# Cross-attention on one Trainium2 core: the four weighted-sum blocks of a batch moved into one block of the next iteration

## The chip, the cores and the metric

The kernel runs on one core of a Trainium2 chip (trn2). The metric is the device time of one execution in microseconds, as the median of several runs. The profile shows one execution by itself; its own time and its span are given beside the median below.

## The reference, cut to what matters

One pre-norm decoder layer in float32 on x of shape (32, 100, 256): self-attention (16 heads of 64), cross-attention to a context of (32, 361, 256) (16 heads of 16), and a routed feed-forward layer with 8 experts. The change is in cross-attention alone, which computes for each of the 32 batches:

```python
q = split_heads(h @ Wq.T + bq)      # h = layernorm(x): 100 rows, 16 heads of 16
k = split_heads(ctx @ Wk.T + bk)    # 361 rows
v = split_heads(ctx @ Wv.T + bv)
scores = einsum('bhqd,bhkd->bhqk', q, k) / sqrt(16)
attn = softmax(where(mask == 0, -inf, scores))
out = einsum('bhqk,bhkd->bhqd', attn, v)
x = x + out.reshape(B, 100, 256) @ Wo.T + bo
```

## The kernel before

The kernel is one program with stages in a row: self-attention, `cross_attention`, routing, `experts`. Each engine runs its own instruction stream, ordered by hand, and the streams meet through semaphores. In `cross_attention` all five streams loop over the 32 batches with `over_batches` (L1529): batches 0 and 1 and the last four are written out, 2 to 27 run in a loop of two batches a turn.

The loop is a software pipeline. In its step for batch b the TensorE stream (`step`, L1457) makes

- the keys and queries of batch b + 2 (`keys` L1354 in two halves, `queries` L1345) and, at the end, the transposed input of batch b + 3 (`turn_x`);
- the scores of batch b + 1, one head at a time (`scores` L1382, called by `maximum_of`), 100 queries by 362 keys in one matmul, only so that VectorE can take the row maxima. They alternate between two PSUM banks, and head h waits for the maximum of head h - 2 (L1385);
- the shifted and transposed scores of batch b (`shifted` L1390), from which ScalarE makes the probabilities with an exponential (`exps` L1130). There are 12 of these tiles a batch: four quarters of heads (u = 0 to 3) by three blocks of keys (kt = 0 to 2). They alternate between two PSUM banks too. The negated maxima enter as a row of the queries by a DMA that ScalarE issues (`maxima` L1119); the shifted scores of quarters 0 and 2 wait for it (L1393);
- the values of batch b + 1 in three blocks (`values` L1364);
- the weighted sums (`weighted` L1401): for a quarter of heads, three key blocks by four heads, each a small matmul with 32 columns of weights that writes one of four groups of 32 PSUM partitions. The profile shows a quarter's 12 calls as 24 matmuls;
- the output of batch b - 1 (`turn_raw`, `turn_out`, `project`).

The weighted sums of quarter 0, 1 and 2 of batch b stand in its own step, behind heads 6, 10 and 14 of the next batch's scores; quarter 3 of batch b - 1 stands in step b behind the transposed maxima. The probabilities lie in two buffers, quarter u in buffer u % 2, so the exponentials of a quarter wait for the weighted sums of two quarters before (L1132).

VectorE (`step`, L1286) takes the 16 row maxima (L1244), and between them the low bits of keys (L1227) and queries (L1234), layer-norm statistics (L1214, L1217), the quotients (L1253, L1255), the normalised input (L1222), the routing statistics (L1268) and the residual (L1262), in a fixed order. ScalarE makes high bits of keys (L1107) and queries, exponentials and copies. GpSimd splits the context of batch b + 3 into high and low bits (`split_context`, L1036 and L1038) once the values of batch b + 1 are done; the keys need it (L1357). SP stores the packed keys and queries of batch b + 2 to DRAM and loads them back in two halves (`place`, L1007); heads 0 and 8 wait for a half each (L1384).

Of the kernel before, what the change touches and what calls it, by code (L numbers as in the profile page):

```python
# [11 lines left out]
ACT = mybir.ActivationFunctionType  # L12
AX_X = mybir.AxisListType.X

B, S, D = 32, 100, 256
# [19 lines left out]
KT = [121, 121, 119]  # L35
# [62 lines left out]
def reach(eng, semaphore, value):  # L98

    if isinstance(value, int) and value <= 0:  # L100
        return
    eng.wait_ge(semaphore, value)
# [691 lines left out]
def cross_attention(nc, c, ctxT, wo, bo, kb_dram, kd, qd, ones_dram):  # L794
# [12 lines left out]
    with ExitStack() as ctx:  # L807
        def sb(name, shape, dt=F32):
            return ctx.enter_context(nc.sbuf_tensor(name, shape, dt))

        def psum(name, shape, dt=F32):
            return ctx.enter_context(nc.psum_tensor(name, shape, dt))

        def sem(name):
            return ctx.enter_context(nc.semaphore(name))

        KP = KT[0]
# [19 lines left out]
        v_ext = sb("v_ext2", [KP, 2, 3, H2, 32])  # L837
        row_max = sb("row_max2", [S, 2, H2])
        neg_max = sb("neg_max", [HG, 2, S], F32R)
        probs = sb("probs2", [KP, 2, 3, 4 * S])  # L840
        recip = sb("recip2", [S, H2])
        o_raw = sb("o_raw", [128, 4 * S])
        o_norm = sb("o_norm2", [S, D])
# [4 lines left out]
        ps_t = [psum(f"psb_t{i}", [128, 512]) for i in range(2)]  # L848
# [42 lines left out]
        pv_ready = sem("pv2_ready")  # L891
# [51 lines left out]
        def more(b, ahead):  # L943
            return not isinstance(b, int) or b + ahead < B
# [141 lines left out]
        def _(act):  # L1086
# [42 lines left out]

            def exps(b, u, kt):  # L1130
                if kt == 0:
                    reach(act, pv_ready, b * 4 + (u - 1))  # L1132
                i = 3 * u + kt
                act.wait_ge(shifted_ready, b * 12 + (i + 1))
                act.sem_inc(act_passed, 1)
                act.activation(probs[0:KT[kt], u % 2, kt], ps_t[i % 2][0:KT[kt], 0:4 * S], ACT.Exp,  # L1136
                               scale=HD2 ** -0.5).then_inc(probs_ready, 1)

            def raw_out(b):
# [191 lines left out]
        def _(pe):  # L1331
# [13 lines left out]
            def queries(b, p):  # L1345
                bank_free(pe, b, Q0)
                pe.wait_ge(xt_copied, fill_of(b, Q0) + 1)
                for g in range(KD):
                    for k in range(KD):
                        ins = pe.matmul(bank(p, Q0)[:, S * g:S * (g + 1)], wq_sb[:, k, 128 * g:128 * (g + 1)],  # L1350
                                        x_t[:, S * k:S * (k + 1)], start=(k == 0), stop=(k == KD - 1))
                ins.then_inc(q_filled, 1)

            def keys(b, p, g):  # L1354
                bank_free(pe, b, KEYS[g])
                if g == 0:
                    pe.wait_ge(c_lo_ready, fill_of(b, K0) + 1)  # L1357
                for k in range(KD):
                    cols = slice(128 * g, 128 * (g + 1))
                    ins = split3(pe, bank(p, KEYS[g])[:, 0:S2E], wk_hi[:, k, cols], wk_lo[:, k, cols],  # L1360
                                 c_hi[:, p, k], c_lo[:, p, k], k == 0, k == KD - 1)
                ins.then_inc(k_filled, 1)
# [10 lines left out]
            def turn_maxima(b, p, half):  # L1373

                f = MT1 if half else MT0
                n, par = fill_of(b, f), p if half else 1 - p
                bank_free(pe, b, f)
                pe.wait_ge(max_ready, n * H2 + (HG * half + HG))
                pe.transpose(bank(p, f)[0:HG, 0:S], row_max[:, par, HG * half:HG * (half + 1)],
                             c.ident[0:S, 0:S]).then_inc(mt_filled, 1)  # L1380

            def scores(b, p, h):  # L1382
                if h % HG == 0:
                    pe.wait_ge(packed[p][h // HG], (b - p) * (PACKS * 8) + PACKS * 16)  # L1384
                reach(pe, max_ready, b * H2 + (h - 1))  # L1385
                u, g, a = h // 4, h // 2 % 2, h % 2
                pe.matmul(ps_s[h % 2][0:S, 0:S2E], q2[0:97, p, u, g, S * a:S * (a + 1)], k2[0:97, p, u, g],  # L1387
                          start=True, stop=True).then_inc(scores_ready, 1)

            def shifted(b, p, u, kt):  # L1390
                i, n = 3 * u + kt, KT[kt]
                reach(pe, probs_ready, b * 12 + (i - 1))
                if i % 6 == 0:  # L1393
                    pe.wait_ge(max_placed[i // 6], b * 16 + 16)
                rows = slice(KT0[kt], KT0[kt] + n)
                for g in range(2):
                    ins = pe.matmul(ps_t[i % 2][0:n, 2 * S * g:2 * S * (g + 1)], k2[:, p, u, g, rows], q2[:, p, u, g],  # L1397
                                    start=True, stop=True)
                ins.then_inc(shifted_ready, 1)

            def weighted(b, p, u):  # L1401
                if u == 0:
                    reach(pe, raw_copied, b)
                    pe.wait_ge(v_copied, b * 3 + 3)
                    pe.wait_ge(live_ready, b + 1)
                for kt in range(3):
                    pe.wait_ge(probs_ready, b * 12 + (3 * u + kt + 1))
                    n = KT[kt]
                    for h in range(4):
                        ins = pe.matmul(ps_o[32 * h:32 * (h + 1), S * u:S * (u + 1)], v_ext[0:n, p, kt, 4 * u + h, :],  # L1410
                                        probs[0:n, u % 2, kt, S * h:S * (h + 1)], start=(kt == 0), stop=(kt == 2))
                ins.then_inc(pv_ready, 1)

            def turn_raw(b):
                pe.wait_ge(raw_copied, b + 1)
                reach(pe, x2_ready, b)
                for u in range(4):
                    ins = pe.transpose(ps_f[0:S, 128 * u:128 * (u + 1)], o_raw[:, S * u:S * (u + 1)], c.ident[:])
                ins.then_inc(raw_turned, 1)
# [37 lines left out]
            def step(b, p):  # L1457
                first = isinstance(b, int) and b == 0
                nxt, next2 = more(b, 1), more(b, 2)

                def maximum_of(*heads):
                    for h in heads:
                        if nxt:
                            scores(b + 1, 1 - p, h)

                shifted(b, p, 0, 0)
                if next2:
                    keys(b, p, 0)
                maximum_of(0)
                shifted(b, p, 0, 1)  # L1470
                if next2:
                    queries(b, p)
                maximum_of(1)
                shifted(b, p, 0, 2)
                if next2:
                    keys(b, p, 1)
                maximum_of(2)
                turn_maxima(b, p, 1)
                if not first:
                    weighted(b - 1, 1 - p, 3)  # L1480
                maximum_of(3)
                shifted(b, p, 1, 0)
                maximum_of(4)
                shifted(b, p, 1, 1)
                maximum_of(5)
                shifted(b, p, 1, 2)
                maximum_of(6)
                weighted(b, p, 0)
                maximum_of(7)
                if not first:  # L1490
                    turn_raw(b - 1)
                shifted(b, p, 2, 0)
                maximum_of(8)
                if nxt:
                    values(b, p, 0)
                shifted(b, p, 2, 1)
                maximum_of(9)
                if nxt:
                    turn_maxima(b, p, 0)
                    values(b, p, 1)  # L1500
                shifted(b, p, 2, 2)
                maximum_of(10)
                weighted(b, p, 1)
                if not first:
                    turn_out(b - 1)
                maximum_of(11)
                shifted(b, p, 3, 0)
                if nxt:
                    values(b, p, 2)
                maximum_of(12)  # L1510
                shifted(b, p, 3, 1)
                maximum_of(13)
                if not first:
                    project(b - 1)
                if more(b, 3):
                    turn_x(b, p)
                shifted(b, p, 3, 2)
                maximum_of(14)
                weighted(b, p, 2)
                maximum_of(15)  # L1520

            over_batches(pe, step)
            weighted(B - 1, 1, 3)
            turn_raw(B - 1)
            turn_out(B - 1)
            project(B - 1)
# [2 lines left out]
def over_batches(eng, emit):  # L1529

    emit(0, 0)
    emit(1, 1)
    with eng.Fori(1, B // 2 - 2) as i:
        emit(i * 2, 0)
        emit(i * 2 + 1, 1)
    for b in range(B - 4, B):
        emit(b, b % 2)
# [635 lines left out]
```

## Time and profile before

| | |
|---|---|
| median of 3 runs | 1639.34 us (1637.56 to 1639.75) |
| the profiled execution | 1636.23 us |
| its span, first to last instruction | 1634.5 us |
| mean granted TensorE clock | 0.947 of full speed |
| TensorE matmuls busy | 1444.6 us (88%) |
| VectorE busy | 963.9 us (59%) |
| ScalarE busy | 758.2 us (46%) |
| GpSimd busy | 557.3 us (34%) |
| cross-attention in the span | about 690 to 1218 us |

PE is TensorE's matmuls, PEld its weight loads, DVE VectorE, ACT ScalarE, POOL GpSimd, SP the queue that issues most DMAs. Tiles go by the program's names with the buffer numbers left out: `psb_s` are the scores' banks, `psb_t` those of the shifted scores, `psb_o` the weighted sums, `psb_p` the projections. Lines L52 to L54 are the three matmuls of a split-precision product: with `wk` among the operands they are keys, with `wv` values. In a timeline a row starts with the time from the span's start and the duration, both in us; "x24" means 24 instructions merged, and the bracket gives the idle time of the engine before it and what ended it.

### The profile page before, as it was taken

The page shows a single profiled execution, that of the slowest core. Times are in us where ns is not written, and L with a number is a line of the kernel's source. Part 1 is how long each engine was busy: PE and PEld are TensorE (multiplying, and loading weights), DVE is VectorE, ACT ScalarE, POOL GpSimd, SP SyncE. Part 2 cuts the span into 40 slices and gives each one's busy share as a digit, 9 for nine tenths or more (in the row PEclk, how much of TensorE's full clock was granted, in tenths as well). Part 3 has the DMA queues.
Part 4 walks back from the last instruction along what each step waited for, and adds up shares of the span by engine and source line. Part 5 has one row for each costly group of instructions (what it writes and reads, how often), then busy time and mean ns, then how long its engine had stood idle before and what let it go on. Part 6 is the DMA issues. An engine that isn't in the chain of part 4 may idle for free. (4 is left out here: it accounts for less than half of the span.)

```text
span 1634.5 us, 39265 instructions
## 1 busy us (share of the span) xinstructions
PE 1444.6 (88%) x12244; PEld 1249.5 (76%) x12244; DVE 963.9 (59%) x2371; ACT 758.2 (46%) x1830; POOL 557.3 (34%) x690
## 2 busy tenths in 40 slices
PE   4899899999999999599999999999977029999997
PEld 3688878888787878578888888888867028888886
DVE  5647474756666655367777777777752225555553
ACT  4547474646555565146555555555541002222221
POOL 5244343525252616322222222222201443333332
PEclk9999999999999999689999999999995559999999
DMA  5813030303021211377676667676621514555551
GB/s 183 238 25 82 1 80 0 80 10 70 22 59 30 50 41 43 98 200 187 190 185 189 186 189 188 186 191 184 177 58 49 151 53 157 178 173 189 183 184 52
DMA packets 160098, 195.82 MB, mean 120 GB/s; under 512 B 83742, under 2 KB 128453, under 8 KB 159782
## 3 DMA queue, kind: packets, MB, share of 16 engines
q1 hardware_dynamic: 154504, 186.19, 41.5%
q0 software_dynamic: 3968, 6.59, 1.3%
q10 hardware_dynamic: 1568, 2.30, 0.5%
q8 instruction: 32, 0.52, 0.1%
q14 instruction: 26, 0.21, 0.0%
HBM read 138.67 MB, written 58.11 MB: 120 GB/s over the span
## 5 line engine op out<-in xcount | busy, mean ns | idle before, releaser
L1244 DVE TENSOR_REDUCE row_max<-psb_s 100x1 f32<-100x361 f32 x512 | 263.4, 531 | 140.3 <-PE psb_s L1387 134.4
L1136 ACT ACTIVATE probs<-psb_t 121x400 f32<-121x400 f32 (+1 forms) x384 | 190.3, 507 | 114.7 <-PE psb_t L1397 112.0
L1387 PE MATMUL psb_s<-k,q 97*100 97x362 f32 x512 | 185.4, 364 | 15.4 <-DVE row_max L1244 9.5
L510 POOL TENSOR_TENSOR diag<-neg_ident,row_max 100x400 fp32r<-100x400 f32 x128 | 112.0, 896 | 184.3 <-DVE row_max L603 153.9
L1397 PE MATMUL psb_t<-q,k 98*121 98x200 f32 (+1 forms) x768 | 147.1, 274 | 2.1 <-ACT probs L1136 1.7
L2079 PE MATMUL psd_y<-w_sb,hid 128*128 128x256 f32 x640 | 144.5, 379 | 0.0
L2071 PE MATMUL psd_h<-h_in,w_sb 128*128 128x256 f32 x640 | 143.0, 382 | 1.4 <-ACT h_in L1937 1.4
L2071 PEld LDWEIGHTS psd_h<-h_in,w_sb 128*128 128x128 f32 x640 | 122.6, 192 | 18.6 <-issue 1.8
L2079 PEld LDWEIGHTS psd_y<-w_sb,hid 128*128 128x128 f32 x640 | 120.1, 190 | 15.5
L1397 PEld LDWEIGHTS psb_t<-q,k 98*121 98x121 f32 (+1 forms) x768 | 125.4, 184 | 6.2 <-ACT probs L1136 2.7
L1387 PEld LDWEIGHTS psb_s<-k,q 97*100 97x100 f32 x512 | 86.0, 168 | 41.4 <-DVE row_max L1244 27.4
L1952 ACT ACTIVATE hid<-psd_h,b_sb 128x256 f32<-128x256 f32 x100 | 47.3, 473 | 146.0 <-PE psd_h L2071 146.0
L426 ACT ACTIVATE probs<-ps_t 100x400 f32<-100x400 f32 x128 | 57.5, 501 | 111.7 <-PE ps_t L751 111.7
L1410 PE MATMUL psb_o<-probs,v_ext 121*32 121x100 f32 (+1 forms) x3072 | 92.5, 253 | 0.0
L1912 POOL DMA_INDIRECT out<-res,token x40 | 40.9, 1023 | 151.3 <-DVE res L2039 145.2
L292 ACT COPY q_t<-ps_p 64x200 f32<-64x200 f32 x112 | 57.0, 509 | 73.4 <-PE ps_p L54 72.6
L52 PE MATMUL ps_p<-x_lo,w_hi 128*128 128x400 f32 x224 | 82.6, 369 | 4.7 <-DVE q_t L292 0.6
L496 POOL CAST o_hi<-stage 128x400 fp32r<-128x400 f32 x64 | 59.1, 924 | 76.9 <-ACT stage L436 40.8
L1937 ACT ACTIVATE h_in<-psd_x,bet,gam 128x256 f32<-128x256 f32 x40 | 20.4, 560 | 139.6 <-PE psd_x L2051 139.6
L436 ACT COPY stage<-ps_ot 64x200 f32<-64x200 f32 x256 | 81.8, 320 | 6.0 <-PE ps_ot L761 1.2
L603 DVE TENSOR_REDUCE row_max<-ps_s 100x4 f32<-100x400 f32 x128 | 67.6, 571 | 28.4 <-PE ps_s L707 27.9
L498 POOL TENSOR_TENSOR o_lo<-stage,o_hi 128x400 fp32r<-128x400 f32 x64 | 81.9, 1280 | 5.1
(226 smaller groups left out, 3596.1 us busy)
## 6 DMA issues: line engine op xcount, KB each, us to landing
w_sb<-in_w SPq DMA_DIRECT2D x40, 1024.0 KB, 7.7
packed_keys<-k_st SPq DMA_DIRECT2D x32, 724.0 KB, 3.6
k<-packed_keys SPq DMA_DIRECT2D x64, 362.0 KB
v_rows<-v_tok SPq DMA_DIRECT2D x32, 400.0 KB
v_ext<-v_rows SPq DMA_DIRECT2D x32, 400.0 KB
q<-packed_queries SPq DMA_DIRECT2D x64, 200.0 KB
k<-packed_keys SPq DMA_DIRECT2D x64, 181.0 KB
packed_queries<-q_st SPq DMA_DIRECT2D x128, 50.0 KB, 2.6
```

What stands on the lines that cost most here:

```text
L52: pe.matmul(out, hi_l, lo_r, start=first, stop=False)
L436: act.copy(*turned_part(r - 2, a, odd)).then_inc(ot_copied_act, 1)
L498: pool.tensor_tensor(lo, src, hi.bitcast(F32), ALU.subtract).then_inc(o_lo_ready, 1)
L510: pool.tensor_tensor(diag[:, g % 2], c.neg_ident[0:S, 0:S].unsqueeze(1).to_broadcast([S, GH, S]), row_max[:, g // 2 % 2, g % 2].unsqueeze( ...
L603: dve.reduce_max(row_max[:, r % 2, :, 2 * n:2 * n + 2].rearrange("p g h -> p h g"), ps_s[n][0:S, :].rearrange("p (h j) -> p h j", h=2)[:, ...
L1136: act.activation(probs[0:KT[kt], u % 2, kt], ps_t[i % 2][0:KT[kt], 0:4 * S], ACT.Exp, scale=HD2 ** -0.5).then_inc(probs_ready, 1)
L1244: dve.reduce_max(row_max[:, p, h:h + 1], ps_s[h % 2][0:S, 0:S2], AX_X).then_inc(max_ready, 1)
L1387: pe.matmul(ps_s[h % 2][0:S, 0:S2E], q2[0:97, p, u, g, S * a:S * (a + 1)], k2[0:97, p, u, g], start=True, stop=True).then_inc(scores_ready, 1)
L1397: ins = pe.matmul(ps_t[i % 2][0:n, 2 * S * g:2 * S * (g + 1)], k2[:, p, u, g, rows], q2[:, p, u, g], start=True, stop=True)
L1410: ins = pe.matmul(ps_o[32 * h:32 * (h + 1), S * u:S * (u + 1)], v_ext[0:n, p, kt, 4 * u + h, :], probs[0:n, u % 2, kt, S * h:S * (h + 1)], ...
L2071: ins = pe.matmul(ps_h[f % 4][:, 0:T], c.w1_sb[:, p, k, 128 * f:128 * (f + 1)], h_in[:, p, k], start=(k == 0), stop=(k == KD - 1))
L2079: ins = pe.matmul(ps_y[t][:, 0:D], hid[:, f, 128 * t:128 * (t + 1)], c.w2_sb[:, p, f, :], start=(f == 0), stop=(f == NF - 1))
```

## The change

The four quarters' weighted sums of batch b - 1 now stand together in step b, right behind head 0's scores; after the last batch its four quarters follow together. Each quarter has a probabilities buffer of its own, so the exponentials of quarter u wait for the weighted sums of the same quarter of the batch before.

```diff
-        probs = sb("probs2", [KP, 2, 3, 4 * S])
+        probs = sb("probs2", [KP, 4, 3, 4 * S])
...
             def exps(b, u, kt):
                 if kt == 0:
-                    reach(act, pv_ready, b * 4 + (u - 1))
+                    reach(act, pv_ready, b * 4 + (u - 3))
...
-                act.activation(probs[0:KT[kt], u % 2, kt], ps_t[i % 2][0:KT[kt], 0:4 * S], ACT.Exp,
+                act.activation(probs[0:KT[kt], u, kt], ps_t[i % 2][0:KT[kt], 0:4 * S], ACT.Exp,
...
-                                        probs[0:n, u % 2, kt, S * h:S * (h + 1)], start=(kt == 0), stop=(kt == 2))
+                                        probs[0:n, u, kt, S * h:S * (h + 1)], start=(kt == 0), stop=(kt == 2))
...
                 maximum_of(0)
+                if not first:
+                    for u in range(4):
+                        weighted(b - 1, 1 - p, u)
                 shifted(b, p, 0, 1)
...
                 turn_maxima(b, p, 1)
-                if not first:
-                    weighted(b - 1, 1 - p, 3)
                 maximum_of(3)
...
                 maximum_of(6)
-                weighted(b, p, 0)
                 maximum_of(7)
...
                 maximum_of(10)
-                weighted(b, p, 1)
                 if not first:
                     turn_out(b - 1)
...
                 maximum_of(14)
-                weighted(b, p, 2)
                 maximum_of(15)

             over_batches(pe, step)
-            weighted(B - 1, 1, 3)
+            for u in range(4):
+                weighted(B - 1, 1, u)
             turn_raw(B - 1)
```

## Rows read from the trace of the kernel before

**Rows 1.** The page's first part: busy us, share of the span, instructions.

```profile
PE 1444.6 (88%) x12244; PEld 1249.5 (76%) x12244; DVE 963.9 (59%) x2371; ACT 758.2 (46%) x1830; POOL 557.3 (34%) x690
```

**Rows 2.** Windows, all of cross-attention: stretch, busy by engine (PE, PEld, DVE, ACT, POOL), clock, DMA.

```profile
690.00:1218.00 528.00, 512.10 (x5958) 434.54 (x5959) 370.21 (x843) 305.36 (x787) 119.71 (x180) 0.99 0.67 181
```

**Rows 3.** List of waits, 720 to 1200 us: total us, times, longest.

```profile
PEld psb_s L1387 <- DVE row_max L1244: 20.6, 60, 0.4
```

**Rows 4.** PE's timeline: one steady batch, and one row of batch 30.

```profile
900.58 0.33 PE L1387 MATMUL psb_s<-k,q 97*100 97x362 f32 x1
900.75 0.36 PE L1397 MATMUL psb_t<-q,k 98*121 98x200 f32 x2
...
903.59 0.72 PE L1410 MATMUL psb_o<-probs,v_ext 121*32 121x100 f32 x24
...
906.22 0.72 PE L1410 MATMUL psb_o<-probs,v_ext 121*32 121x100 f32 x24
...
910.75 0.72 PE L1410 MATMUL psb_o<-probs,v_ext 121*32 121x100 f32 x24
...
912.00 0.29 PE L52 MATMUL psb_p<-wv_lo,c_hi 128*119 128x256 f32 x1
...
914.53 0.33 PE L1387 MATMUL psb_s<-k,q 97*100 97x362 f32 x1
914.79 0.72 PE L1410 MATMUL psb_o<-probs,v_ext 121*32 121x100 f32 x24
...
915.69 0.36 PE L1397 MATMUL psb_t<-q,k 98*121 98x200 f32 x2
915.89 0.34 PE L52 MATMUL psb_p<-c_lo,wk_hi 128*128 128x362 f32 x1
...
916.92 0.33 PE L1387 MATMUL psb_s<-k,q 97*100 97x362 f32 x1
...
1198.57 0.43 PE L1397 MATMUL psb_t<-q,k 98*121 98x200 f32 x2 [0.34 <-DMA q<-neg_max]
```

**Rows 5.** Windows, second keys to head 7's scores: batch 0, then a steady batch.

```profile
707.60:712.22 4.62, 3.92 (x44) 2.97 (x42) 3.97 (x11) 2.88 (x8) 0.27 (x2) 1.00 0.20 44
902.20:907.07 4.87, 4.57 (x69) 3.48 (x67) 4.11 (x11) 3.27 (x9) 0.34 (x2) 1.00 0.84 211
```

**Rows 6.** DVE's timeline: batch 0 (709 to 710), then a steady batch.

```profile
709.55 0.58 DVE L1227 SCALAR_TENSOR_TENSOR k_st<-psb_p,stage,k_st 128x362 fp32r<-128x362 f32 x1
710.05 0.96 DVE L1244 TENSOR_REDUCE row_max<-psb_s 100x1 f32<-100x361 f32 x2
...
904.17 0.58 DVE L1227 SCALAR_TENSOR_TENSOR k_st<-psb_p,stage,k_st 128x362 fp32r<-128x362 f32 x1
904.81 0.97 DVE L1244 TENSOR_REDUCE row_max<-psb_s 100x1 f32<-100x361 f32 x2
905.70 0.42 DVE L1214 BATCH_NORM_STATS2 stats<-x_all 100x6 f32 x1
...
906.48 0.97 DVE L1244 TENSOR_REDUCE row_max<-psb_s 100x1 f32<-100x361 f32 x2
```

**Rows 7.** PEld's timeline (weight loads), the same steady batch.

```profile
907.07 0.16 PEld L1387 LDWEIGHTS psb_s<-k,q 97*100 97x100 f32 x1 [0.35 <-DVE row_max L1244]
...
914.79 0.50 PEld L1410 LDWEIGHTS psb_o<-probs,v_ext 121*32 121x32 f32 x24 [0.18 <-issue]
```

**Rows 8.** PE's timeline at the end of cross-attention: quarters 2 and 3 together.

```profile
1215.93 1.24 PE L1410 MATMUL psb_o<-probs,v_ext 121*32 121x100 f32 x48
```

**Rows 9.** POOL's timeline, the same steady batch: the split of the context.

```profile
914.01 1.59 POOL L1038 TENSOR_TENSOR c_lo<-c_t,c_hi 128x722 fp32r<-128x722 f32 x1
```

**Rows 10.** PE's timeline, batch 0: third value block, then the next keys.

```profile
716.68 0.29 PE L52 MATMUL psb_p<-wv_lo,c_hi 128*119 128x256 f32 x1
...
720.35 0.41 PE L52 MATMUL psb_p<-c_lo,wk_hi 128*128 128x362 f32 x1 [0.27 <-POOL c_lo L1038]
```

**Rows 11.** Windows, the same columns as rows 2: the DMA queues when a steady batch ends.

```profile
914.00:914.60 0.60, 0.60 (x7) 0.53 (x5) 0.34 (x2) 0.09 (x1) 0.59 (x1) 1.00 0.00 0
```

## The prediction

> **What bounds the kernel now.** I read the page first, then the windows of the cross-attention stage, the list of waits, and last the timelines of one batch. The page's engine line [rows 1] gives TensorE 88% of the span. Inside cross-attention it is busier still: 512 of 528 us, at a clock share of 0.99 [rows 2]. The Trainium skill ("Trainium Kernel Development and Optimization", Performance Expectations) calls matmul busy time a bad measure, because matmuls are pipelined; the trace agrees, since 4.57 us of a 4.87 us stretch count as busy [rows 5] although weight loads stand idle in it. So a busy TensorE may still be waiting, and I went on to the waits. TensorE's weight loads wait 20.6 us in all for VectorE's row maxima [rows 3], always in the same part of a batch. From one batch to the next, head 0's score matmul goes from 900.58 to 916.92 [rows 4]: 16.34 us a batch, 32 batches.
>
> A batch has two kinds of stretch. From the second key matmuls (902.20) to head 7's scores (907.07), 4.87 us [rows 5], VectorE sets the pace: its low bits of the keys start at 904.17, two maxima follow at 904.81, the batch-norm statistics at 905.70, two maxima at 906.48 [rows 6], and head 7's scores start at 907.07, after 0.35 us of idleness that ended with a maximum [rows 7]. The scores have two banks, so head 7 must wait for head 5's maximum (L1385). Everywhere else TensorE works nearly without a pause and sets the time.
>
> The four weighted blocks stand at 903.59 (quarter 3 of the batch before), 906.22 (quarter 0), 910.75 and 914.79 (quarters 1 and 2) [rows 4]. **The first two lie in VectorE's stretch, the last two in TensorE's.**
>
> **What a block costs.** Alone: from head 14's scores (914.53) to the shifted scores (915.69) is 1.16 us [rows 4]; it holds two score matmuls at 0.17 each (900.58 to 900.75), so the block takes 0.83 on TensorE with both its transitions. I use the same for quarter 1. A second block behind another: the kernel's end has the only pair, 48 matmuls in 1.24 us [rows 8] where 24 take 0.72 [rows 4], so 0.52 us. Four in one block: 0.83 + 3 x 0.52 = 2.39 us. Its 192 instructions in a row are not seen before; the pair is the nearest row, and I take its rate. The bounds are 0.52 and 0.83 for each further one.
>
> Why a lone block is dearer: its weight load starts with its first matmul at 914.79, after 0.18 us idle [rows 7], where other loads run ahead. The Trainium skill ("TensorEngine Tiling (Array Packing)", Tiling Modes, Key Properties) has the rule: changing the tiling mode drains the array. The trace agrees with it: 0.83 against 0.52 is 0.31 a switch. By that rule alone three switches a batch would go and the change would win; the rows below speak against it.
>
> **The change, part by part, for batches 1 to 29:**
>
> 1. The block of four goes in behind head 0's scores, before the second shifted scores. That is TensorE's own stretch (900.58 to 902.20 holds no wait): **+2.39 us**. Its operands are long ready, the last probabilities being from the batch before.
>
> 2. Quarters 3 and 0 leave VectorE's stretch. TensorE has 1.66 us less to do there, but the chain of VectorE starts with the second keys and stays: keys (TensorE), high bits (ScalarE), low bits, two maxima, statistics, maximum, head 7's scores. The first batch is the test that the old kernel contains: it has no quarter 3 in that stretch, and its stretch still takes 4.62 us against 4.87 [rows 5]. The 0.25 comes from head 3's maximum, which there starts 0.50 us behind the low bits (709.55, 710.05) and 0.64 in the steady batch (904.17, 904.81) [rows 6], and from small pauses. So **-0.25**, not -1.66. Quarter 0 in that first stretch is then cover that TensorE waits behind anyway; bounds: 0 and -1.66. What is late next is nothing new: the same VectorE chain, with TensorE idle some 1.9 us in it instead of 0.5.
>
> 3. Quarter 1 leaves TensorE's stretch: **-0.83**. VectorE idles behind it, and its consumers (raw copy, quotients) now belong to the batch before and are early.
>
> 4. Quarter 2 leaves the stretch from the third value block (912.00) to the first keys of the next batch (915.89), 3.89 us [rows 4]. Without it TensorE would need 3.06. But GpSimd splits the next context there, only after that value block: its subtraction starts at 914.01 and takes 1.59, to 915.60 [rows 9]. In the first batch that chain did decide: value block at 716.68, keys at 720.35 after a wait of 0.27 for it [rows 10], 3.67 us. So the stretch can shrink to 3.67 only: **-0.22**, not -0.83. The wait of 0.61 is new, with the keys and all scores behind it. Bounds: -0.83 and 0.
>
> 5. ScalarE's first exponential now waits for the block's first quarter (the four buffers make it wait for quarter 0 of the batch before, which is read some 1 us after it would start). Behind it on ScalarE stands the copy of the keys' high bits, and behind that VectorE's low bits; TensorE needs them only for the second keys (their bank), which come behind the block's 2.39 us. That covers it: 0. Uncovered it would cost about that 1 us a batch.
>
> 6. DMA: no transfer is added. But stores of queries and keys, and so the load of the first half of the packed keys, start 2.39 us later in the batch, on SP's queue too, where the loads of the second half are behind them. In the old kernel the DMA queues are empty from 914.00 [rows 11] and head 0 of the next batch starts at 916.92, 2.9 us on. The batch grows by 1.1, so the spare falls to about 1.6: 0. The negated maxima of the first half come for the next shifted scores; a late one costs at most what step 4 does not hide. In the last batch but one such a wait shows already, 0.34 [rows 4]. Probability buffers take more space and no time.
>
> Sum for a batch: 2.39 - 0.25 - 0.83 - 0.22 = **+1.09 us; x 29 = +31.6**. Batch 0 has no block and already waits for the split: -0.83. Batch 30 has no keys or statistics; its quarters 3 and 0 lie before the wait for the maxima's DMA (the 0.34): 2.39 - 2 x 0.83 = +0.73. Behind batch 31 the end becomes four blocks instead of two (+1.04), in front of it stand 2.39, and one of its own blocks was in the way: together +2.6. **Total +34.1 us.** The profiled execution took 1636.2 (span 1634.5 and 1.7 around it), so 1670.3 for it; it lies 3.1 below the median of the runs, 1639.34. On the median: **1673.4**.
>
> **Rivals.** *The switches decide (faster).* If heads 3 to 7 are not held by VectorE once the blocks are out, all four lone blocks (3.32) turn into 2.39: -0.93 a batch; with the split's wait +0.61 that is -0.32, in all 1630 us; without it 1611. For it: TensorE counts as busy through the stretch. Against: the first batch's 4.62 and the 0.35 us idles. It decides if more than 1.34 of the 1.66 us come back from that stretch. 6%. *No measurable change:* VectorE's chain gives back about 1.1 us more than I take, in 29 batches, about 1640; the first batch shows nothing like it. 4%.
> *The split is hidden:* quarter 2 gives its whole 0.83, so +0.48 a batch: 1656. Against: 3.67 was measured. 8%.
> *The packed keys come late:* the load now meets the second half's traffic; 2 us later than I say costs 0.4 us a batch, 1685. For it: a DMA share of 0.84 in the stretch at 902 [rows 5]. 10%.
> *The long block is not fed:* each further quarter costs between 0.52 and 0.83, at the middle +0.46 a batch, 1687, at the end 1702. Against: the pair ran at the full rate. 6%.
> *The change does not do what it says* has no room here: the blocks move, visibly.
>
> **The numbers.** The forecast, with 66%, has a range of its own of 1662 to 1683 (errors of 0.35 us a batch in steps 2 and 4). With the hidden split below and the late keys above, 1655 to 1690 holds a little over 8 in 10. About 0.2% (3 us) is what a measurement of this kernel can tell from no change. Slower by more than that: 66 + 8 + 10 + 6 = 90%; within it 4%; faster 6%.
>
> **What would show it.** One group of 96 matmuls of the weighted sums a batch, about 2.3 us long (step 1). From the second keys to head 7's scores 4.6 to 4.9 us, with the waits of TensorE's weight loads for the row maxima up from 0.7 to about 2 us a batch (step 2). From the third value block to the first keys 3.7 us, and a new wait of TensorE for GpSimd's split of some 0.6 us a batch (step 4). A batch of 17.4 us. The forecast is wrong if the stretch to head 7 falls under 4 us, if the block takes 2.7 us or more, or if a wait for the packed keys shows.

## The result and the profile after

The changed kernel takes **1688.46 us** in the median (4 runs, 1686.11 to 1692.84) against 1638.45 for the kernel before in the same comparison: ratio 1.0308, 95% interval 1.0285 to 1.0331, so 50 us slower. The forecast was 1673.4, slower by 34, with a range to 1690: the sign and the mechanism held, the size was a third too small.

For the changed kernel, the page's engine line and the windows of the stretch from the second keys to head 7's scores in two batches in a row (columns: stretch, its length, busy PE, PEld, DVE, ACT, POOL, clock, DMA share, GB/s):

```profile
PE 1463.6 (87%) x12244; PEld 1269.3 (75%) x12244; DVE 958.2 (57%) x2371; ACT 750.5 (44%) x1830; POOL 557.0 (33%) x690
...
906.39:911.08 4.69, 3.49 (x20) 2.50 (x18) 4.01 (x11) 3.26 (x9) 0.34 (x2) 1.00 0.39 97
925.24:929.94 4.70, 3.50 (x21) 2.52 (x19) 4.02 (x11) 3.27 (x9) 0.35 (x2) 1.00 0.47 102
```

These answer to [rows 5]: the stretch still takes 4.70 us, although TensorE is now busy for 3.50 of it instead of 4.57. VectorE is busy for 4.02 us of it, where it was 4.11. TensorE's timeline of two changed batches, with the transposes of maxima (L1379) that mark a batch's length:

```profile
907.57 0.25 PE L1379 MATMUL psb_p<-ident,row_max 100*8 100x100 f32 x1
...
916.47 0.29 PE L52 MATMUL psb_p<-wv_lo,c_hi 128*119 128x256 f32 x1
...
920.12 0.43 PE L52 MATMUL psb_p<-c_lo,wk_hi 128*128 128x362 f32 x1 [0.37 <-POOL c_lo L1038]
...
921.22 0.33 PE L1387 MATMUL psb_s<-k,q 97*100 97x362 f32 x1
921.48 2.28 PE L1410 MATMUL psb_o<-probs,v_ext 121*32 121x100 f32 x96
923.69 0.46 PE L1397 MATMUL psb_t<-q,k 98*121 98x200 f32 x2
...
925.24 0.34 PE L52 MATMUL psb_p<-c_lo,wk_hi 128*128 128x362 f32 x1
926.43 0.25 PE L1379 MATMUL psb_p<-ident,row_max 100*8 100x100 f32 x1
...
929.94 0.42 PE L1387 MATMUL psb_s<-k,q 97*100 97x362 f32 x1 [0.56 <-DVE row_max L1244]
...
934.05 0.29 PE L52 MATMUL psb_p<-wv_lo,c_hi 128*119 128x256 f32 x1
...
944.07 0.25 PE L1379 MATMUL psb_p<-ident,row_max 100*8 100x100 f32 x1
```

Cut at the same instructions as [rows 4], a batch before and a batch after (from the third values at 916.47 to those at 934.05) compare like this (us; the last column is what the prediction's steps made of each part):

| part of a batch | before | after | predicted |
|---|---|---|---|
| head 0's scores and the block of four | 0.17 | 2.47 | 2.56 |
| to the second keys | 1.45 | 1.55 | 1.45 |
| second keys to head 7's scores | 4.87 | 4.70 | 4.62 |
| head 7's scores to the third values | 4.93 | 4.11 | 4.10 |
| third values to the first keys | 3.89 | 3.65 | 3.67 |
| first keys to head 0's scores | 1.03 | 1.10 | 1.03 |
| sum | 16.34 | 17.58 | 17.43 |

So all of the predicted terms are there. What no step had stands in the length of the batches: 926.43 to 944.07 is 17.64, but 907.57 to 926.43 is **18.86**, and so is every fourth batch of this execution. Windows of the same work, from the first to the third shifted scores of quarter 2, in a long and in a short batch:

```profile
911.69:915.56 3.87, 3.87 (x22) 3.72 (x20) 2.71 (x7) 1.50 (x4) 0.70 (x2) 0.56 0.87 243
930.55:933.14 2.59, 2.58 (x23) 2.27 (x20) 2.56 (x7) 1.44 (x4) 0.69 (x2) 1.00 0.91 290
```

The same matmuls take 3.87 us instead of 2.59, and the granted clock is 0.56 instead of 1.00: nearly the whole of this stretch ran at 1.2 GHz instead of 2.4. Seven batches of the steady part have such a fall, always right behind the stretch in which TensorE idles; the kernel before has none there. Together they are 7 x 1.25 = 8.8 us of the profiled execution. That execution is also the slowest of the four runs. Three more falls, and a wait for the packed keys at head 0's scores of batch 31, belong to the stage's end; the wait in TensorE's timeline:

```profile
1242.50 0.41 PE L1387 MATMUL psb_s<-k,q 97*100 97x362 f32 x1 [1.53 <-DMA k<-packed_keys]
```

Last, the list of waits of the changed kernel, 720 to 1200 us:

```profile
PEld psb_s L1387 <- DVE row_max L1244: 47.6, 83, 1.0
DVE k_st L1227 <- ACT k_st L1107: 33.8, 27, 1.5
...
ACT probs L1136 <- PE psb_o L1410: 74.9, 27, 3.4
...
PEld psb_t L1397 <- DMA q<-neg_max: 7.6, 18, 0.7
...
PE psb_p L52 <- POOL c_lo L1038: 6.8, 20, 0.8
```

TensorE's weight loads wait 47.6 us for row maxima where [rows 3] had 20.6, with 83 waits instead of 60. ScalarE's wait for the block (74.9) and VectorE's behind it (33.8) are new and large; whether they cost anything is tried below. The wait for GpSimd's split is the one of step 4. The one for the negated maxima's DMA, 18 times in 27 batches, is new as well: the list of the kernel before has a single one, of 0.3 us.

### The profile page after: what moved, and what is told of

Its sections match the earlier page's. It is cut to its first block and busy times, and to the rows that moved or that the text cites. A ratio compares the mean times of both kernels' runs of the same rounds, so it can differ in the third digit from the quotient of the medians.

```text
span 1691.1 us, 39395 instructions
## 1 busy us (share of the span) xinstructions
PE 1463.6 (87%) x12244; PEld 1269.3 (75%) x12244; DVE 958.2 (57%) x2371; ACT 750.5 (44%) x1830; POOL 557.0 (33%) x690
## 5 line engine op out<-in xcount | busy, mean ns | idle before, releaser
L1244 DVE TENSOR_REDUCE row_max<-psb_s 100x1 f32<-100x361 f32 x512 | 257.3, 529 | 158.7 <-PE psb_s L1387 150.2
L1387 PE MATMUL psb_s<-k,q 97*100 97x362 f32 x512 | 177.8, 369 | 41.3 <-DVE row_max L1244 37.5
L1397 PE MATMUL psb_t<-q,k 98*121 98x200 f32 (+1 forms) x768 | 156.2, 286 | 6.2 <-ACT probs L1136 2.3
L1951 ACT ACTIVATE hid<-psd_h,b_sb 128x256 f32<-128x256 f32 x100 | 47.4, 474 | 147.2 <-PE psd_h L2070 146.0
L1044 POOL TENSOR_SCALAR var_eps<-mv 100x1 f32<-100x1 f32 x32 | 7.5, 236 | 277.8 <-DVE mv L1217 277.8
```

What stands on the lines that cost most here:

```text
L1244: dve.reduce_max(row_max[:, p, h:h + 1], ps_s[h % 2][0:S, 0:S2], AX_X).then_inc(max_ready, 1)
```

## The experiments

Times are medians; "a batch" is read from the transposes of maxima in each trace. The kernel before was timed again with each group of runs (medians 1638.45 to 1640.16), and the ratios compare within a group; a difference between medians of two groups is known to some 2 us only.

### Old places, four buffers

```diff
-        probs = sb("probs2", [KP, 2, 3, 4 * S])
+        probs = sb("probs2", [KP, 4, 3, 4 * S])
...
-                    reach(act, pv_ready, b * 4 + (u - 1))
+                    reach(act, pv_ready, b * 4 + (u - 3))
```

(and `u` for `u % 2` in the two uses; the blocks stay where they were)

> The kernel before with four probabilities buffers and the exponentials' later wait, the blocks left in their old places. My theory (the place of the blocks decides, the buffers do nothing): 1639 us, a batch of 16.3. Rival (the larger buffers or the other wait of ScalarE cost something by themselves): 1645 or more.

Measured 1637.48 us, ratio 0.9998 (0.9983 to 1.0013), a batch of 16.3:

```profile
901.65 0.25 PE L1379 MATMUL psb_p<-ident,row_max 100*8 100x100 f32 x1
...
917.95 0.25 PE L1379 MATMUL psb_p<-ident,row_max 100*8 100x100 f32 x1
```

The buffers do nothing by themselves; the place of the blocks is the whole loss.

### The block in VectorE's stretch

```diff
                 maximum_of(0)
-                if not first:
-                    for u in range(4):
-                        weighted(b - 1, 1 - p, u)
                 shifted(b, p, 0, 1)
...
                 shifted(b, p, 1, 1)
+                if not first:
+                    for u in range(4):
+                        weighted(b - 1, 1 - p, u)
                 maximum_of(5)
```

With four buffers the engines would wait for each other for ever (the third shifted scores need the first exponential, and that needs the block), so there are eight: quarter u of batch b in buffer 4 (b % 2) + u.

> The block of four stands behind the shifted scores of quarter 1's second key block, inside the stretch that VectorE paces, instead of behind head 0's scores; eight probabilities buffers make that order possible. Theory of the stretches: from the second keys to head 7's scores about 5.4 us (VectorE's chain runs beside the block), 5.4 - 4.70 = +0.7 there and -2.3 in TensorE's own stretch, so 17.6 becomes 16.0 a batch, and without the idle time there is no fall of the clock: about 1625 to 1635 us, at or below the kernel before. Rival (a long block costs what it costs wherever it stands, because of its instructions or the clock): it stays near 1688.

Measured 1647.48 us, ratio 1.0048 (1.0025 to 1.0071): 41 us less than the changed kernel, with the same instructions in the same block of four. A batch takes 16.5, and the steady part has no fall of the clock but one, at 753 us. TensorE's timeline of the stretch, and its window:

```profile
880.09 0.38 PE L52 MATMUL psb_p<-c_lo,wk_hi 128*128 128x362 f32 x1
...
882.19 0.41 PE L1390 MATMUL psb_s<-k,q 97*100 97x362 f32 x1 [0.26 <-DVE row_max L1247]
...
882.73 2.28 PE L1413 MATMUL psb_o<-probs,v_ext 121*32 121x100 f32 x96
884.95 0.40 PE L1390 MATMUL psb_s<-k,q 97*100 97x362 f32 x1
...
886.09 0.41 PE L1390 MATMUL psb_s<-k,q 97*100 97x362 f32 x1 [0.37 <-DVE row_max L1247]
```

```profile
880.09:886.09 6.00, 5.36 (x117) 4.58 (x115) 4.02 (x11) 3.08 (x9) 1.53 (x4) 1.00 0.90 246
```

The block adds 6.00 - 4.70 = 1.3 us here and took 2.3 in front. I had expected 0.7: VectorE finishes its queue at 884.2, and head 5's scores (884.95), issued only after the block, restart it only at 885.50, after 1.31 us of idleness; so two waits of TensorE (0.26 before the block, 0.37 after) stay. The rival, that a long block costs the same anywhere, is out. The forecast of 1625 to 1635, at or below the kernel before, was missed for that 0.6 a batch.

### Statistics early

```diff
                 if more(b, 2):
                     keys(b + 2, p, 0)
+                if more(b, 3):
+                    norm_stats(b + 3)
                 if nxt:
                     maxima(b + 1, 1 - p, 1, 2)
...
                     maxima(b + 1, 1 - p, 3, 5)
-                if more(b, 3):
-                    norm_stats(b + 3)
```

(in VectorE's stream, on top of the change)

> The changed kernel with VectorE's batch-norm statistics moved out of its chain, to behind the first keys' low bits, where VectorE idles beside the block. Theory (VectorE's chain sets the stretch from the second keys to head 7): the stretch goes from 4.70 to about 3.9 us, -0.8 a batch, some 25 us, and with less idle time also fewer falls of the clock: 1655 to 1665. Rival (TensorE or ScalarE sets that stretch): no change, 1688.

Measured 1668.02 us, ratio to before 1.0172 (1.0149 to 1.0195), 20 us less than the changed kernel, and no fall of the clock in the steady part:

```profile
900.12 0.25 PE L1379 MATMUL psb_p<-ident,row_max 100*8 100x100 f32 x1
...
917.16 0.25 PE L1379 MATMUL psb_p<-ident,row_max 100*8 100x100 f32 x1
```

This batch took 17.04, the steady ones 17.09 on average. Not one instruction of TensorE was touched: VectorE's chain sets the stretch. It gave 0.53 a batch rather than 0.8, about 15 of the 20 us; the rest goes with the falls of the clock. TensorE's wait of 0.56 in front of head 7 is gone; those in front of heads 4 and 5 (0.23 and 0.33, in the changed kernel 0.22 and 0.33) do not hang on the statistics and stay.

### The idle time filled

```diff
+            def fill(b, n):
+                if isinstance(b, int) and b == 0:
+                    return
+                reach(pe, x2_ready, b - 1)
+                for _ in range(n):
+                    pe.transpose(ps_f[:, 0:S], c.neg_ident[0:S, :], c.ident[0:S, 0:S])
...
                 shifted(b, p, 1, 0)
+                fill(b, 2)
                 maximum_of(4)
                 shifted(b, p, 1, 1)
+                fill(b, 3)
                 maximum_of(5)
+                fill(b, 1)
                 shifted(b, p, 1, 2)
                 maximum_of(6)
+                fill(b, 6)
                 maximum_of(7)
```

> The changed kernel with 12 transposes of a constant (about 0.11 us each, results unused) put where TensorE idles before heads 4, 5 and 7; they add work and take none away. Theory that the idle time brings the clock down (one batch in four has 3.41 us at half clock and takes 18.87 instead of 17.6): the falls inside the steady batches vanish, all take 17.6 to 17.7, and the time falls by 5 to 10 us in spite of the added work. Rival (the falls come from something else, or the added work is paid for): the falls stay and the time rises by up to 1.3 x 30 = 39 us.

Measured 1679.18 us (1677.71 to 1679.83), ratio to before 1.0240 (1.0219 to 1.0261): 9.3 us less than the changed kernel, with 372 useless matmuls more. TensorE's timeline of the stretch:

```profile
901.80 0.34 PE L52 MATMUL psb_p<-c_lo,wk_hi 128*128 128x362 f32 x1
...
903.49 0.34 PE L1419 MATMUL psb_f<-ident,neg_ident 100*128 100x100 f32 x2
903.88 0.41 PE L1387 MATMUL psb_s<-k,q 97*100 97x362 f32 x1
...
904.33 0.42 PE L1419 MATMUL psb_f<-ident,neg_ident 100*128 100x100 f32 x3
...
905.07 0.25 PE L1419 MATMUL psb_f<-ident,neg_ident 100*128 100x100 f32 x1
...
905.74 0.68 PE L1419 MATMUL psb_f<-ident,neg_ident 100*128 100x100 f32 x6
906.50 0.41 PE L1387 MATMUL psb_s<-k,q 97*100 97x362 f32 x1
```

901.80 to 906.50 is 4.70 us, as without the filling: so much of TensorE's time in this stretch is free. That is step 2 of the prediction laid bare. And the falls are gone from the steady part. Windows of 770 to 1220 us in this run, in the changed kernel, and in the run below with a shorter split and no filling:

```profile
770.00:1220.00 450.00, 436.26 (x5143) 377.28 (x5142) 294.70 (x686) 238.72 (x637) 102.82 (x154) 1.00 0.64 172
```

```profile
770.00:1220.00 450.00, 411.63 (x4711) 353.87 (x4711) 290.94 (x678) 236.93 (x628) 99.62 (x150) 0.97 0.63 170
```

```profile
770.00:1220.00 450.00, 417.24 (x4849) 361.78 (x4847) 297.08 (x690) 241.20 (x640) 77.93 (x153) 0.97 0.65 173
```

### Eight buffers

The changed kernel with the eight buffers of the second experiment; `reach(act, pv_ready, b * 4 + (u - 7))`.

> The changed kernel with eight probabilities buffers, so that ScalarE's first exponential of a batch no longer waits for the block (it stands idle 2.7 us there, and the high bits of the first keys behind it). My step 5 says that the block covers this wait: no change, 1688, a batch of 17.6. Rival (the wait delays keys and maxima and is part of the loss): 0.2 us a batch or more come back, 1680 or less.

Measured 1688.45 us, ratio 1.0310 (1.0284 to 1.0336): the changed kernel's time. (The four runs of each spread over 7 to 8 us, so that the medians agree to 0.01 us is luck.) The 75 us of ScalarE's waits for the block are gone from the list, and nothing comes back. The largest new wait of the profile costs nothing, as step 5 had it.

### The split cut short

```diff
-            pool.memset(c_lo[:, :, :, S2:S2E].bitcast(F32), 0.0).then_inc(pad_ready, 1)
+            pool.memset(c_lo[:, :, :, 120:S2E].bitcast(F32), 0.0).then_inc(pad_ready, 1)
...
-                pool.tensor_tensor(c_lo[:, p, :, 0:S2], c_t[p], c_hi[:, p, :, 0:S2].bitcast(F32),
+                pool.tensor_tensor(c_lo[:, p, :, 0:120], c_t[p][:, :, 0:120], c_hi[:, p, :, 0:120].bitcast(F32),
                                    ALU.subtract).then_inc(c_lo_ready, 1)
```

> The changed kernel with GpSimd's subtraction of the context split done for 120 of 361 columns (the low bits of the rest are left at zero), so that the split ends about 1 us earlier. My step 4 says that TensorE waits for it 0.6 us a batch since quarter 2 is gone: the stretch from the third value block to the next keys goes from 3.65 to about 3.1, the batch from 17.6 to 17.0 or 17.1, and the median to 1665 to 1675 (less idle time may also save falls of the clock). Rival (the wait only hides one for the negated maxima's DMA behind it, which is late too): 0.1 to 0.2 us a batch, 1683 or more.

Measured 1681.58 us, ratio to before 1.0254 (1.0230 to 1.0277), 6.9 less than the changed kernel: between the two forecasts. GpSimd's subtraction takes 0.66 instead of 1.59 us, and no keys wait for it any more. TensorE's timeline of the part from the third values to the first keys, in two batches, and the weight load that waits in the second:

```profile
913.42 0.30 PE L52 MATMUL psb_p<-wv_lo,c_hi 128*119 128x256 f32 x1
...
916.50 0.35 PE L52 MATMUL psb_p<-c_lo,wk_hi 128*128 128x362 f32 x1
...
930.49 0.29 PE L52 MATMUL psb_p<-wv_lo,c_hi 128*119 128x256 f32 x1
...
933.89 0.35 PE L52 MATMUL psb_p<-c_lo,wk_hi 128*128 128x362 f32 x1
```

```profile
933.59 0.29 PEld L1397 LDWEIGHTS psb_t<-q,k 98*121 98x121 f32 x2 [0.43 <-DMA q<-neg_max]
```

The first is 3.08, the 3.06 of step 4; the second 3.40, held by the negated maxima's DMA. Of the 3.65 us of the changed kernel 0.57 come back in some batches and 0.25 in others, so theory and rival are each half right. And the falls of the clock became more, not fewer: the trace has ten in the steady part (not nine, as the expectation of the last run below says) where the changed kernel has seven. A batch with a fall takes about 18.3 us here and one without 17.3, so the three more eat some 3 us of the gain.

### Quarter 3 later, with and without the statistics early

```diff
                 turn_maxima(b, p, 1)
-                if not first:
-                    weighted(b - 1, 1 - p, 3)
                 maximum_of(3)
                 shifted(b, p, 1, 0)
                 maximum_of(4)
                 shifted(b, p, 1, 1)
+                if not first:
+                    weighted(b - 1, 1 - p, 3)
                 maximum_of(5)
```

(the kernel before, two buffers; the second of the two also has the statistics behind the first keys' low bits)

> The kernel before with one edit: quarter 3 stands behind the shifted scores of quarter 1's second key block, where TensorE waits for a maximum, instead of in front of head 3's scores. Theory of the stretches: head 3's scores come earlier, VectorE starts its maximum 0.50 instead of 0.64 behind the low bits, and the wait of 0.34 in front of head 5 is filled: the stretch from the second keys to head 7 goes from 4.87 to about 4.6 to 4.7, 1631 to 1634. Rival (VectorE's statistics and maxima fill the stretch whatever TensorE does, or the raw copy now comes late): 1639 or more.

> The same as the run with quarter 3 later, and the batch-norm statistics moved behind the first keys' low bits. Theory: with 0.78 us out of VectorE's chain TensorE itself sets the stretch, about 4.4 us instead of 4.87, 15.85 a batch, 1624 to 1628, faster than the kernel before. Rival (the chain is not VectorE's): no more than the run without the statistics' move.

Measured 1656.80 us (ratio 1.0109, 1.0088 to 1.0129) and 1659.35 (1.0119, 1.0100 to 1.0138): both slower, and both expectations wrong. I had overlooked the exponentials' wait. TensorE's timeline and ScalarE's, of the run without the statistics' move:

```profile
910.23 0.72 PE L1410 MATMUL psb_o<-probs,v_ext 121*32 121x100 f32 x24
...
911.76 0.46 PE L1397 MATMUL psb_t<-q,k 98*119 98x200 f32 x2 [0.46 <-ACT probs L1136]
```

```profile
911.20 0.50 ACT L1136 ACTIVATE probs<-psb_t 121x400 f32<-121x400 f32 x1 [1.69 <-PE psb_o L1410]
```

Quarter 1's exponential overwrites the buffer of quarter 3 of the batch before, so with two buffers it waits for the block, and the shifted scores after it wait for the PSUM bank that this exponential frees. Here nothing covers ScalarE's wait, and a batch takes 16.8 us, 0.5 more. It is the kind of wait that step 5 was about, there at a quarter that the block of four covers.

### The same with four buffers

> The kernel before with four probabilities buffers and quarter 3 behind the shifted scores of quarter 1's second key block. With two buffers the same move made the exponential of quarter 1 wait for quarter 3, and TensorE for that exponential (0.46 us in front of the third shifted scores, 16.8 a batch). Theory: four buffers take that wait away, the wait in front of head 5 is filled, and the stretch from the second keys to head 7 falls below 4.87: 15.9 to 16.15 a batch, 1627 to 1635. Rival (VectorE fills the stretch, so the move brings nothing once the new wait is gone): 16.3, 1639.

> The same with the batch-norm statistics moved behind the first keys' low bits. Theory: VectorE's chain is then 0.78 us shorter and TensorE sets the stretch, 4.4 to 4.6 us, 15.8 to 16.0 a batch, 1623 to 1630, the fastest of all. Rival (what is left is TensorE's own work already in the run without the statistics' move): no difference between the two.

Measured 1634.54 us, **ratio 0.9975 (0.9965 to 0.9985)**, and 1643.19, ratio 1.0026 (1.0012 to 1.0040). The first is faster than both kernels, by 4 us against the kernel before: small, but outside the noise. It has the four buffers of the change and one quarter moved by a few instructions. Its batch and its stretch to head 7's scores:

```profile
900.01 0.25 PE L1379 MATMUL psb_p<-ident,row_max 100*8 100x100 f32 x1
...
916.16 0.25 PE L1379 MATMUL psb_p<-ident,row_max 100*8 100x100 f32 x1
```

```profile
914.95:919.67 4.72, 4.46 (x68) 3.54 (x66) 4.01 (x11) 3.34 (x9) 0.34 (x2) 1.00 0.83 215
```

A batch takes 16.15, and the stretch 4.72 instead of 4.87; the weight load of head 7's scores waits 0.16 us for a row maximum where it waited 0.35 [rows 7]. 1634.5 is the slow edge of what I expected. With the statistics moved as well a batch takes 16.4: the move is a loss here, and that expectation (1623 to 1630, the fastest of all) was wrong. TensorE's timeline of that run:

```profile
908.23 0.25 PE L1379 MATMUL psb_p<-ident,row_max 100*8 100x100 f32 x1 [0.25 <-DVE q_st L1234]
```

In front of the first queries VectorE has no block to hide behind, so the statistics make the queries' low bits late, and the transposed maxima, which reuse their PSUM bank, wait for them. The same edit that won 20 us in the changed kernel costs 9 in this one.

### Short split and filled idle time

> The changed kernel with both the short split (120 of 361 columns of the context's low bits) and the 12 transposes of a constant in TensorE's idle time. With the short split alone the batches were 17.05 to 17.45 and nine falls of the clock in the steady part added about 1.2 us each. Theory (idle time in VectorE's stretch brings the clock down, filled it does not): no falls in the steady part, every batch 17.1 to 17.4, about 1666 to 1671. Rival (the falls come with the short waits elsewhere): they stay, 1680.

Measured 1669.75 us, ratio 1.0182 (1.0160 to 1.0205): 11.8 less than the short split alone, by the filling only. No fall in the steady part:

```profile
770.00:1220.00 450.00, 440.86 (x5210) 383.37 (x5210) 301.50 (x701) 244.17 (x652) 78.54 (x154) 1.00 0.66 176
```

## Why the prediction was right, and what it lacked

**Step 1**, +2.39 for the block: 2.30 in the table. The long block ran at the pair's rate (2.28 us for 96 matmuls, [rows 8] plus two times 0.52), so the rival of the starved block is out. The lower rate of a lone block is as read from the rows; what is saved on three of them a batch is real, and worth less than the cover lost. That the difference is the switch of tiling mode is the prediction's reading: no run here varied the switches by themselves.

**Step 2**, the stretch does not shrink by the 1.66 us of work taken out: right, 4.70, and shown twice: 1.3 us of useless matmuls fit in without lengthening it, and moving VectorE's statistics alone took 0.53 us off each batch.

**Step 3** right (0.82). **Step 4** right in size, 3.65 against 3.67, but the split is not alone there: the list has the wait for the negated maxima's DMA 18 times in 27 batches, and with the split cut short that DMA still held back 0.32 of the 0.57 us in one of the two batches shown. **Step 5** right: eight buffers change nothing. **Step 6** right in the steady part, not at the end: the prediction named a wait for the packed keys as a sign of being wrong, and one came, of 1.53 us, in the last batch but one, where I had put nothing for it (1.07 us in the run with eight buffers).

The size failed in two places. First, a **term that the sum lacked**: step 2 said "TensorE idle some 1.9 us in it instead of 0.5" and priced that idleness at nothing beyond itself. It brings the clock down in every fourth batch, 1.25 us each time; filling it took the falls away and gave back 9.3 us in the median. No row of the kernel before shows such a fall in the steady part (both stretches of [rows 5] are at 1.00), so the price was unseen, and an unseen price wanted a bound, not a zero. Second, the **sum for a batch, +1.09**, came out as about +1.33. The table has 0.15 more than the steps (the first matmuls behind the block and behind the wait for GpSimd cost 0.07 to 0.10 more, and the stretch 0.08 over the first batch's 4.62), and the batch I started from, 16.34, was one of the longer ones: the mean of the 29 intervals in the trace before is 16.26. 29 x 0.24 = 7 us. With 34 predicted, 9 for the clock and 7 for the batches the sum is 50, the measured difference. That it closes so well is in part luck, since the terms come from one trace and the difference is one of medians. Within the two traces the 29 intervals are 47.2 us longer (31.6 + 7 + 8.8 = 47.4), while the profiled executions are 56.6 us apart; of the rest 3.4 lie in the last two batches, with the wait for the packed keys and the last falls, and the others before the first batch's mark and behind the last one's. I had 2.5 for both ends together, and no experiment looked at them.

## What to carry to other kernels

Work that stands where an engine waits for another can be free, as long as it fits into the wait and nothing else waits for it: the transposes cost nothing there, the block of four 1.3 of its 2.3 us, and quarter 3, with two buffers, held up an exponential. Before gathering pieces to save a fixed cost per piece, find for each whether its place is one where its engine waits, and keep them there. The test is cheap: put useless work in that place and see whether the time moves. When a change makes TensorE idle more often, price the clock as well as the wait, and read several periods of the loop, since what the clock does need not show in each.

## What the runs showed that I had not expected

TensorE's clock falls although no single wait is long. The timeline of the changed kernel's weight loads in the stretch before the fall at 912, and its window over 520 us:

```profile
908.47 0.16 PEld L1387 LDWEIGHTS psb_s<-k,q 97*100 97x100 f32 x1 [0.41 <-DVE row_max L1244]
909.41 0.16 PEld L1387 LDWEIGHTS psb_s<-k,q 97*100 97x100 f32 x1 [0.51 <-DVE row_max L1244]
...
911.08 0.16 PEld L1387 LDWEIGHTS psb_s<-k,q 97*100 97x100 f32 x1 [0.85 <-DVE row_max L1244]
```

```profile
720.00:1240.00 520.00, 475.19 (x5458) 408.57 (x5456) 335.94 (x781) 274.33 (x727) 114.80 (x172) 0.98 0.63 170
```

The longest idle times are 0.41, 0.51 and 0.85 us, TensorE is still busy for 475 of 520 us, and yet the granted clock went to half behind that stretch in every fourth batch (0.56 against 1.00 in the windows above), and with 1.3 us a batch of constant transposes in the gaps it did not, in two pairs of kernels (1688.5 and 1679.2; 1681.6 and 1669.8). The Trainium skill ("TensorE: Matmul & The Clock Gate", A second HAM failure mode: psum-queue depth-cycling) describes such an oscillation for short, frequent idle times between groups of matmuls; these runs agree with it: the clock changes between 1.00 and half although no wait of the weight loads in the list of 720 to 1200 us is longer than 1.0 us. Why three of four batches with the same idle time are spared stays open: in the run with the short split the falls came in pairs, two batches in a row and then four or five without, and with eight buffers they came every third or fourth batch, so their rhythm is not the loop's, and no run here settles what sets it.

A smaller thing: the block costs a little on the way out too. The pair of shifted scores behind it takes 0.46 us (923.69), where the same pair took 0.36 behind head 0's scores (900.75 in [rows 4]). Such a pair takes 0.46 also behind a wait (909.86 in the changed kernel, after 0.29 us without a weight load), so no run here tells whether the block's narrow weights or the late weight load is the reason.
